# Score matmuls parted around the block matmuls, whole blocks in the last batch, and another order at the program's end

## The chip, the cores and the metric

The kernel runs on one core of a Trainium2 chip. The metric is the device time of one execution in microseconds (us). TensorE (PE) multiplies matrices, with weight loads (PEld) that can run beside it; VectorE (DVE), ScalarE (ACT) and GpSimd (POOL) work on tiles in the on-chip memory; SyncE (SP) issues transfers. All engines take their instructions in program order and wait for each other through semaphores.

## The reference

Eight sequences of 1024 tokens with 256 features go through one layer, all in float32: attention with 16 heads of 16, then a gated feed-forward that mixes each token with the one before it.

```python
x = x + _layernorm(attn(_layernorm(x)))      # softmax(q k^T / 4) v, then w_o
x = x + _layernorm(ffn(_layernorm(x)))
# ffn(x): x_prev = x shifted by one token
# xr = mu_r*x + (1-mu_r)*x_prev ; xk = mu_k*x + (1-mu_k)*x_prev
# sigmoid(xr W_r^T) * ((relu(xk W_k^T)**2) W_v^T)
```

## The kernel before

The work is cut into 16 half batches `u` (8 batches of 2 x 512 queries) of 32 steps `s` each, 512 steps `i` in all. A step handles four heads (`qd`), 512 queries (`hf`) and 128 keys (`kt`). On TensorE a step consists of three things, in this order:

- `scores(i + 1)` (L567): for each of two pairs `p` two matmuls (L577) into the bank pair `PS[p]`, one on rows 0 to 49 and one on rows 64 to 113 of the array, which run side by side. They wait for the exponential of the same pair a step earlier, since it reads the same bank. Each pair has one exponential on ScalarE (L584), 128 x 1024, into `PT`.
- `pump` (L302): a piece of everything else that needs TensorE. That work is cut into blocks. A `Block` is a projection of 128 x 512 or 2 x 128 x 256 outputs in three products of high and low halves, which stand in for float32 (Q, K, V of the next batch: "ahead"; y = w_o, k, r, v of the feed-forward of the half batch before: "behind"). Its contraction over 128 rows is parted into two halves of 64 rows: half 0 on rows 0 to 63, half 1 on rows 64 to 127. `begin` (L255) sends half 0 of a new block beside half 1 of the one before, so that two blocks overlap; each `step_part` (L284) sends half of such a tile, so a tile takes two steps. A `Turn` (`turn`, L243) is four transposes of 128 x 128 and is sent at once. `choose(age)` (L219) takes the first block of each chain that has been ready, and a bank of three that has been free, for `age` steps; the bank freed first is taken first. `pump` sends two pieces in a step where `left` is 0 (steps 0 to 8 of the first half batch).
- `values(i)` (L589): four matmuls (L596; float32, two passes each) on all 128 rows and four column groups of 32, into the accumulator `PO`, after both exponentials of step i.

When a block's last matmul is sent, its `done` queues the work on the other engines; at a `yield REST` it pauses, and goes on one step later. `norm_stats` (L651) computes mean and variance on VectorE and the inverse root on GpSimd (L657, L658), `normed` (L661) applies them. Words name blocks: `Q00` is Q, feature half 0, token half 0; `T10` a transpose of the normalized input, token half 1; `y0 y1`, `z0 z1` (transposes), `k`, `r`, `v` the feed-forward's. The lists `FIRST`, `EVEN`, `ODD` (L828 to L830) give their order; in the last batch, which has none ahead, only "behind" words are left.

Before the loop, `run` (L869) sends the first batch's work: `p_direct` (D and E words, L459) writes the first heads' queries and keys straight into `QS` and `KS`, with a copy on ScalarE (L466) and a subtraction on VectorE (L469). The list `meanwhile` gives small works that are queued after each of these blocks. `keep_warm(n)` (L168) sends n matmuls whose result nobody reads.

After the loop the last half batch's y, z, k, r, v run alone (L978), each on all 128 rows, with fillers (L981) between them: a number in the list of words is so many matmuls that nobody reads. Before each word `rest_no_more` queues all work that is pausing.

Of the kernel before, what the change touches and what calls it, by code (L numbers as in the profile page):

```python
# [56 lines left out]
def sandwich_kernel(nc, x, wpack, consts, out):  # L57
    with ExitStack() as ctx:
# [129 lines left out]
        class Block:  # L188
# [3 lines left out]
            def __init__(self, chain, half, ready, done, queued=(), tokens=None):  # L192
                self.chain, self.half, self.ready, self.done = chain, half, ready, done
                self.seen, self.queued, self.tokens = None, queued, tokens

# [58 lines left out]

        def begin(age):  # L255

            took[:] = 0.0, 0.0
            block = choose(age)
            if isinstance(block, Turn):
                turn(block)  # L260
                return False
            now[:] = block, now[0]
            if now[0] is not None:
                tile[0] = queue(now[0].half(PM[now[0].bank[0]], 0), *now[0].waits[0])
            if now[1] is not None:
                tile[1] = queue(now[1].half(PM[now[1].bank[0]], 1), now[1].token)
            return bool(tile[0] or tile[1])
# [15 lines left out]

        def step_part(age):  # L284


            fresh = not (tile[0] or tile[1])
            if fresh and not begin(age):
                return
            ends = [None, None]  # L290
            limit = [sum(op[0] for op in tile[a]) / 2 - .03 if fresh else 1e9 for a in range(2)]
            emit(*limit, ends)
            if ends[0] is not None:
                now[0].token = ends[0]
            if ends[1] is not None:
                block = now[1]
                now[1] = None
                until_rest(block.done(block.bank[0], PM[block.bank[0]], ends[1]))

        doubled = [False]  # L300

        def pump(left, age=1):  # L302

            for block in waiting:
                if block.seen is None and block.ready() is not None:
                    block.seen = step_now[0]
            need = sum(block.cost for block in waiting) + bool(tile[0] or tile[1])
            step_part(age)
            doubled[0] = not doubled[0] and need > left and step_now[0] % 32 > 9
            if doubled[0] or not left:  # L310
                step_part(age)

# [146 lines left out]
        def p_direct(i, p, n):  # L459
            cols, dst = slice(n * 512, n * 512 + 512), (QS, KS)[i][0]  # L460

            def done(k, m, tok):
                state["qk_read"] = tk["B_read"] = tok
                for a in range(2):
                    rows = slice(64 * a, 64 * a + SHIFT)
                    h = act.op(lambda e, rows=rows: e.activation(dst[rows, p, cols], m[rows, :], ACT.Copy), tok)  # L466
                for a in range(2):
                    rows = slice(64 * a + 32 * i, 64 * a + 32 * i + 16)
                    d = dve.op(lambda e, rows=rows: e.tensor_tensor(dst[rows, p, cols], m[rows, :],  # L469
                                                                    dst[rows, p, cols].bitcast(F32), ALU.subtract), h)  # L470
                free_bank(k, d)
                here.setdefault((0, 0, i, n), []).append(d)
                if meanwhile:
                    meanwhile.pop(0)()
# [91 lines left out]
        steps = [(b, qd, hf, kt) for b in range(B) for hf in range(2) for qd in range(4) for kt in range(8)]  # L566
        def scores(i):  # L567
            b, qd, hf, kt = steps[i]
            if kt == 0:
                maxima(b, qd, hf)  # L570
            for p in range(2):
                waits = [rows_all, *here[b, qd, 0, hf], *here[b, qd, 1, kt // 4]]
# [255 lines left out]
        FIRST = "Q00 K00 V2 K01 V3 Q10 K10 K11 Q01 Q11"  # L828
        EVEN = "W3 T00 T01 y0 y1 Q00 T10 T11 z0 z1 k0 k1 r0 r1 v0 v1 K00 Q01 K01"
        ODD = "y0 y1 z0 z1 k0 k1 r0 r1 v0 v1 Q10 K10 Q11 K11 V0 V1 V2"  # L830
# [82 lines left out]
        def sum_all():  # L913
# [5 lines left out]

        meanwhile[:] = [lambda: ln1_norm(0, 1), lambda: (split_weights(["wv"]), sum_heads()),  # L920
                       sum_all, lambda: None, lambda: split_weights(["wq", "wk"])]
        run("D00 E00 D10 E10 T10 T11 V0 V1 E01 E11")
        flagged, = flagging
        load_xa(1)
        scores(0)
        copier[0] = "dve"

        for u in range(2 * B):
# [6 lines left out]
            for s in range(32):  # L935
                i = step_now[0] = 32 * u + s
                if i + 1 < len(steps):
                    scores(i + 1)
                if s == 12:
                    load_xb(u)  # L940
                rested, resting[:] = resting[:], []
                age = 2 if b + 1 == B and 8 <= s < 20 else 1
                pump(0 if u == 0 and s < 9 else 32 - s, age)
                values(i)
# [32 lines left out]
        idle = xA[:, 0:2, :].rearrange("p t c -> p (t c)")  # L977
        for word in "5 y0 y1 11 z0 z1 8 k0 k1 r0 r1 v0 v1".split():  # L978
            if word.isdigit():
# [3 lines left out]
                continue  # L983
            rest_no_more()
            block(B, 2 * B - 1, word)
# [97 lines left out]
```

## Time and profile before

| | us |
|---|---|
| median of 3 runs | 1304.06 (1302.92 to 1306.53) |
| profiled execution | 1305.91 |
| its span, first to last instruction | 1304.1 |
| TensorE busy | 1273.5 (98%) |
| ScalarE busy | 1056.0 (81%) |
| VectorE busy | 783.0 (60%) |
| GpSimd busy | 271.0 (21%) |
| mean granted TensorE clock | 0.987 |

Times are us from the span's start. TensorE's matmuls are pipelined and a row's length includes the tail, so rows overlap; the distance from one start to the next is what an instruction takes of the engine. A clock of 1.00 is 2.4 GHz, 0.50 is 1.2 GHz. "[0.47 <-DVE xnT L409]" says that the engine stood idle 0.47 us before the row and what ended it.

### The profile page before, as it was taken

What the parts mean: (1) busy time and instruction counts of PE and PEld (TensorE: products, weight loads), DVE (VectorE), ACT (ScalarE), POOL (GpSimd) and SP (SyncE); (2) the same over time, 40 slices, a digit from 0 to 9 for tenths busy, and PEclk for the clock granted to TensorE, in tenths of its full rate; (3) what the DMA queues carried; (4) which work ended last, traced back from release to release, by engine and by line L of the source; (5) the groups of instructions that cost most, each with busy time, mean ns of one, the idle gap of its engine ahead of it and who ended that gap; (6) DMA issues with size and microseconds to landing.
All of it is one profiled execution on the core that took longest, in us unless ns stands there. A gap on an engine that the chain in (4) does not pass through costs nothing.

```text
span 1304.1 us, 25655 instructions
## 1 busy us (share of the span) xinstructions
PE 1273.5 (98%) x10694; PEld 647.4 (50%) x10694; DVE 783.0 (60%) x1726; ACT 1056.0 (81%) x1153; POOL 271.0 (21%) x352
## 2 busy tenths in 40 slices
PE   8999999999999999999999999999999999999995
PEld 5543555455545555455544555455554555444353
DVE  5553656758465774857466584747657474545546
ACT  3588888888888888888888888888888888887831
POOL 1000212222211322222121222113221221212210
PEclk8899999999999999999999999999999999998999
DMA  4256383316612194115733176122942056201000
GB/s 149 60 153 189 86 143 82 98 48 127 116 53 81 52 181 95 50 52 113 132 80 98 50 140 121 45 72 82 162 82 66 28 114 132 55 2 33 1 17 17
DMA packets 61798, 112.72 MB, mean 86 GB/s; under 512 B 6512, under 2 KB 31344, under 8 KB 61616
## 3 DMA queue, kind: packets, MB, share of 16 engines
q1 hardware_dynamic: 61360, 109.60, 37.1%
q8 instruction: 102, 1.67, 0.6%
q10 hardware_dynamic: 288, 1.05, 0.2%
q14 instruction: 48, 0.39, 0.1%
HBM read 68.42 MB, written 41.94 MB: 85 GB/s over the span
## 4 chain that ended last, share of the span: by engine, by line
PE 88%; DVE 7%; ACT 3%; POOL 1%; issue 1%; DMA 0%; POOLq 0%; ACTq 0%
PE O L596 36%; PE S L577 25%; PE M L346 14%; PE M L333 10%; PE M L247 3%; ACT PT L584 2%; DVE sth L653 2%; DVE A L662 1%; POOL rsh L658 1%; PE M L480 1%; DMA A<-w_dram 0%; DVE mvh L655 0%; DVE xB L677 0%; DVE T L616 0%; DVE xnT L409 0%
## 5 line engine op out<-in xcount | busy, mean ns | idle before, releaser
L584 ACT ACTIVATE PT<-S 128x1024 f32<-128x1024 f32 x1024 | 991.4, 1023 | 176.9 <-PE S L577 176.9
L596 PE MATMUL O<-PT,V 128*17 128x512 f32 x4096 | 541.3, 600 | 0.0
L577 PEld LDWEIGHTS S<-QS,KS 50*128 50x128 f32 x2048 | 185.6, 184 | 458.4 <-ACT PT L584 410.9
L577 PE MATMUL S<-QS,KS 50*128 50x512 f32 x2048 | 386.8, 452 | 5.8 <-ACT PT L584 5.6
L657 POOL TENSOR_SCALAR veh<-mvh 128x2 f32<-128x2 f32 x96 | 22.3, 232 | 509.4 <-DVE mvh L655 509.4
L596 PEld LDWEIGHTS O<-PT,V 128*17 128x17 f32 x4096 | 67.9, 95 | 104.9 <-issue 62.9
L796 DVE SCALAR_TENSOR_TENSOR A<-Z,M 128x512 f32<-128x512 f32 x30 | 20.4, 682 | 159.0 <-PE M L346 159.0
L333 PE MATMUL M<-xnT,WH 64*128 64x512 f32 x512 | 112.4, 398 | 0.0
L346 PE MATMUL M<-WH,xnT 64*128 64x256 f32 x512 | 86.7, 284 | 0.0
L346 PE MATMUL M<-WH,cT 64*128 64x256 f32 (+1 forms) x496 | 83.7, 282 | 2.8 <-DVE cT L630 2.1
L371 DVE CAST p<-M 128x512 fp32r<-128x512 f32 x62 | 42.4, 684 | 70.5 <-PE M L333 35.6
L346 PE MATMUL M<-WH,C 64*128 64x256 f32 (+1 forms) x496 | 81.7, 278 | 1.0 <-DVE C L760 1.0
L346 PE MATMUL M<-WH,B 64*128 64x256 f32 (+1 forms) x496 | 81.6, 278 | 0.9 <-DVE B L730 0.9
L719 POOL TENSOR_TENSOR C<-A,C 128x512 fp32r<-128x512 f32 x30 | 38.7, 1291 | 155.1 <-DVE C L371 155.1
L658 POOL TENSOR_TENSOR rsh<-veh,half 128x2 f32<-128x2 f32 x96 | 69.1, 720 | 8.0
L333 PEld LDWEIGHTS M<-xnT,WH 64*128 64x128 f32 x512 | 67.1, 189 | 6.8
L333 PE MATMUL M<-xnT,WL 64*128 64x512 f32 x256 | 70.1, 396 | 0.0
L748 POOL TENSOR_TENSOR scratch<-scratch 128x512 f32<-128x512 f32 x30 | 32.8, 1093 | 177.8 <-DVE scratch L746 177.8
L346 PEld LDWEIGHTS M<-WH,xnT 64*128 64x128 f32 x512 | 68.2, 191 | 0.7 <-DVE xnT L409 0.3
L346 PEld LDWEIGHTS M<-WH,cT 64*128 64x128 f32 (+1 forms) x496 | 65.4, 190 | 4.1 <-issue 2.9
L346 PEld LDWEIGHTS M<-WH,C 64*128 64x128 f32 (+1 forms) x496 | 63.6, 185 | 2.9 <-DVE C L760 1.2
L746 DVE TENSOR_SCALAR scratch<-M 128x512 f32<-128x512 f32 x32 | 22.1, 691 | 70.9 <-PE M L333 62.1
(114 smaller groups left out, 1672.5 us busy)
## 6 DMA issues: line engine op xcount, KB each, us to landing
scr<-p SPq DMA_DIRECT2D x124, 256.0 KB
QS<-scr SPq DMA_DIRECT2D x56, 256.0 KB, 6.1
KS<-scr SPq DMA_DIRECT2D x56, 256.0 KB, 10.5
QS<-scr SPq DMA_DIRECT2D x70, 128.0 KB, 6.0
KS<-scr SPq DMA_DIRECT2D x68, 128.0 KB, 8.1
xA<-x_dram SPq DMA_DIRECT2D x16, 512.0 KB, 7.3
xB<-x_dram SPq DMA_DIRECT2D x16, 512.0 KB, 5.2
out_dram<-xB SPq DMA_DIRECT2D x15, 512.0 KB, 3.1
```

The costliest lines, as they stand in the source:

```text
L247: fn = lambda e, t=t: e.transpose(PM[k][:, t * 128:t * 128 + 128], block.src(t), ident[:, :])
L333: out.append((.216, lambda e, k=k, w=w, v=moving(j, c, rows): e.matmul(m[:, :], w, v, start=(a != 1 and k == 0), stop=(a != 0 and k == 5))))
L346: out.append((.117, lambda e, k=k, t=t, w=w, v=still(i, c, t, rows): e.matmul(m[:, t * 256:t * 256 + 256], v, w, start=(a != 1 and k == 0) ...
L371: return dve.op(lambda e: e.tensor_copy(dst, src), *waits)
L577: fn = lambda e, p=p, a=a, rows=rows: e.matmul(PS[p][:, a, :], KS[qd][rows, p, kt * 128:kt * 128 + 128], QS[qd][rows, p, hf * 512:hf * 512 ...
L584: e_fn = lambda e, p=p: e.activation(PT[i % 2][:, 2 * p:2 * p + 2, :], PS[p][:, :, :], ACT.Exp, scale=SCALE)
L596: fn = lambda e, j=j: e.matmul(PO[32 * j:32 * j + 17, :], V[b % 2][:, kt, 4 * qd + j, :], PT[i % 2][:, j, :], start=(kt == 0), stop=(kt == 7))
L653: toks = [dve.op(lambda e, t=t: e.bn_stats(sth[:, 2 * g + t, :], src(t)), *ready) for t in range(2)]
L657: p = pool.op(lambda e: e.tensor_scalar(veh[:, ts], mvh[:, ts, 1], EPS, None, ALU.add), d)
L658: r = pool.op(lambda e: e.tensor_tensor(rsh[:, ts], veh[:, ts], half[:, 0:2], ALU.pow), p)
L719: tk["xk", u, c] = side().op(lambda e: e.tensor_tensor(C[1][:, cols], A[:, cols], C[0][:, cols].bitcast(F32), ALU.subtract), d)
L748: tk["sq", mt] = k1, r, side().op(lambda e: e.tensor_tensor(r[:, :], r[:, :], r[:, :], ALU.mult), d)
```

## The change

- The main loop calls `scores(i + 1, 0)` before `pump` and `scores(i + 1, 1)` from within it, after the block's matmuls. Transposes that were chosen (`turns`) are sent after that.
- In the last batch (`b + 1 == B`) a block runs `solo`: both halves as one, on all 128 rows, in two steps, and no second block beside it. `age` is 2 there for all steps below 20, and no longer for steps 8 to 19 alone.
- `K00` stands before `T11` in `EVEN`.
- In `p_direct`, the copies of the second token half (E01, E11) go to VectorE.
- Two of the `meanwhile` works get warm-up matmuls: one after E00, two after D10.
- At the end there are 9 and 7 fillers instead of 11 and 8, and before `y1` and `v1` the pausing work of `y0` and `v0` isn't queued first: both pieces' later steps then come turn by turn.

```diff
-        def begin(age):
+        def begin(age, turns):
             took[:] = 0.0, 0.0
-            block = choose(age)
+            block = None if solo[0] and now[0] is not None else choose(age)
             if isinstance(block, Turn):
-                turn(block)
+                turns.append(block)
                 return False
             now[:] = block, now[0]
+            if block is not None and now[1] is None and solo[0]:
+                block.solo = True
+                tile[0] = queue(block.half(PM[block.bank[0]], 2), *block.waits[0])
+                return True
...
-            if ends[0] is not None:
+            if ends[0] is not None and now[0].solo:
+                block = now[0]
+                now[0] = None
+                until_rest(block.done(block.bank[0], PM[block.bank[0]], ends[0]))
+            elif ends[0] is not None:
                 now[0].token = ends[0]
...
-        def pump(left, age=1):
+        def pump(left, age=1, between=None):
...
-            step_part(age)
             doubled[0] = not doubled[0] and need > left and step_now[0] % 32 > 9
-            if doubled[0] or not left:
-                step_part(age)
+            turns = []
+            for k in range(2 if doubled[0] or not left else 1):
+                step_part(age, turns)
+            if between is not None:
+                between()
+            for block in turns:
+                turn(block)
...
-                    h = act.op(lambda e, rows=rows: e.activation(dst[rows, p, cols], m[rows, :], ACT.Copy), tok)
+                    if n:
+                        h = dve.op(lambda e, rows=rows: e.tensor_copy(dst[rows, p, cols], m[rows, :]), tok)
+                    else:
+                        h = act.op(lambda e, rows=rows: e.activation(dst[rows, p, cols], m[rows, :], ACT.Copy), tok)
...
-        EVEN = "W3 T00 T01 y0 y1 Q00 T10 T11 z0 z1 k0 k1 r0 r1 v0 v1 K00 Q01 K01"
+        EVEN = "W3 T00 T01 y0 y1 Q00 T10 K00 T11 z0 z1 k0 k1 r0 r1 v0 v1 Q01 K01"
...
-        meanwhile[:] = [lambda: ln1_norm(0, 1), lambda: (split_weights(["wv"]), sum_heads()),
-                       sum_all, lambda: None, lambda: split_weights(["wq", "wk"])]
+        meanwhile[:] = [lambda: ln1_norm(0, 1), lambda: (split_weights(["wv"]), sum_heads(), keep_warm(1)),
+                       lambda: (keep_warm(2), sum_all()), lambda: None, lambda: split_weights(["wq", "wk"])]
...
-                if i + 1 < len(steps):
-                    scores(i + 1)
+                nxt = i + 1 < len(steps)
+                if nxt:
+                    scores(i + 1, 0)
...
-                age = 2 if b + 1 == B and 8 <= s < 20 else 1
-                pump(0 if u == 0 and s < 9 else 32 - s, age)
+                age, solo[0] = (2 if s < 20 else 1, True) if b + 1 == B else (1, False)
+                pump(0 if u == 0 and s < 9 else 32 - s, age, (lambda: scores(i + 1, 1)) if nxt else None)
...
-        for word in "5 y0 y1 11 z0 z1 8 k0 k1 r0 r1 v0 v1".split():
+        for word in "5 y0 y1 9 z0 z1 7 k0 k1 r0 r1 v0 v1".split():
...
-            rest_no_more()
+            if word not in ("y1", "v1"):
+                rest_no_more()
```

## Rows read from the trace of the kernel before

**Rows 1.** Stretches of the span: start:end length, busy us by engine, PEclk, DMA.
```profile
24.60:31.43 6.83, 6.30 (x44) 5.79 (x45) 3.07 (x7) 2.38 (x4) 0.00 (x0) 0.50 0.49 156
39.05:49.67 10.62, 10.50 (x43) 5.17 (x44) 1.16 (x3) 4.72 (x5) 0.00 (x0) 0.56 0.01 2
1102.90:1252.07 149.17, 145.53 (x1151) 67.09 (x1147) 73.88 (x165) 126.71 (x139) 32.75 (x42) 0.98 0.11 26
1252.07:1275.50 23.43, 19.49 (x66) 11.03 (x62) 15.02 (x42) 1.23 (x2) 6.02 (x12) 0.93 0.07 22
1275.50:1304.10 28.60, 16.98 (x84) 11.85 (x84) 17.14 (x36) 5.84 (x10) 1.87 (x4) 0.89 0.06 19
```

**Rows 2.** Timeline of TensorE, one step with a block: start, length, instruction, count.
```profile
601.33 0.72 PE L577 MATMUL S<-QS,KS 50*128 50x512 f32 x4
601.89 0.63 PE L333 MATMUL M<-xnT,WH 64*128 64x512 f32 x4
...
602.68 1.05 PE L596 MATMUL O<-PT,V 128*17 128x512 f32 x8
603.66 0.73 PE L577 MATMUL S<-QS,KS 50*128 50x512 f32 x4
```

**Rows 3.** Timeline of TensorE, scores and block in a step behind an accumulator copy.
```profile
577.79 0.76 PE L577 MATMUL S<-QS,KS 50*128 50x512 f32 x4
578.38 0.39 PE L333 MATMUL M<-xnT,WH 64*128 64x512 f32 x1
```

**Rows 4.** Timeline of TensorE, the step of T11 in an even half batch.
```profile
525.63 0.79 PE L577 MATMUL S<-QS,KS 50*128 50x512 f32 x4
526.89 0.66 PE L247 MATMUL M<-ident,xA 128*128 128x128 f32 x4 [0.47 <-DVE xnT L409]
```

**Rows 5.** Timeline of TensorE, a half block right behind the last values.
```profile
1252.07 0.38 PE L346 MATMUL M<-WH,C 64*128 64x256 f32 x1
1252.29 0.28 PE L346 MATMUL M<-WL,C 64*128 64x256 f32 x1
...
1252.64 0.28 PE L346 MATMUL M<-WL,C 64*128 64x256 f32 x1
```

**Rows 6.** Stretches: four steps with neither block nor transposes; two steps with transposes.
```profile
1126.53:1134.42 7.89, 7.30 (x52) 1.99 (x49) 5.49 (x17) 7.27 (x9) 2.35 (x5) 1.00 0.01 2
1134.42:1139.09 4.67, 4.67 (x36) 1.78 (x33) 1.75 (x7) 4.01 (x5) 0.00 (x0) 1.00 0.00 0
```

**Rows 7.** Timeline of TensorE, the start.
```profile
23.83 0.19 PE L914 MATMUL S<-gsm,ones 128*1 128x2 f32 x2 [2.12 <-DVE gsm L911]
...
26.19 0.79 PE L480 MATMUL M<-xnT,B 64*128 64x512 f32 x1
...
36.22 0.50 PE L577 MATMUL S<-QS,KS 50*128 50x512 f32 x1
...
39.05 1.71 PE L577 MATMUL S<-QS,KS 50*128 50x512 f32 x4 [1.88 <-ACT PT L584]
```

**Rows 8.** Timeline of ScalarE, the first exponentials.
```profile
37.98 3.85 ACT L584 ACTIVATE PT<-S 128x1024 f32<-128x1024 f32 x4
```

**Rows 9.** Timeline of VectorE and ScalarE's copy, from the last values to y1's norm.
```profile
1252.20 0.60 ACT L613 ACTIVATE On<-O 128x512 f32<-128x512 f32 x1 [1.90 <-PE O L596]
...
1254.68 0.68 DVE L616 STREAM_TRANSPOSE T<-On 128x512 f32<-128x512 f32 x1
...
1256.02 0.73 DVE L662 TENSOR_SCALAR A<-A,mvh,rsh 128x256 f32<-128x256 f32 x2
...
1257.40 0.70 DVE L627 STREAM_TRANSPOSE T<-CC 128x512 f32<-128x512 f32 x1
...
1262.09 0.76 DVE L653 BATCH_NORM_STATS2 sth<-M 128x6 f32<-128x256 f32 x2 [2.60 <-PE M L346]
...
1270.85 0.99 DVE L662 TENSOR_SCALAR A<-M,mvh,rsh 128x256 f32<-128x256 f32 x2 [1.14 <-POOL rsh L658]
```

**Rows 10.** Timeline of TensorE, fillers at the end.
```profile
1264.07 9.60 PE L981 MATMUL S<-xA,ident 128*128 128x512 f32 x22
```

## What the change should do to the time

> **What bounds the kernel now.** I first split the span into stretches and read TensorE's busy share and granted clock in each [rows 1]: the middle of the run and the last batch are full of TensorE work, while the end (52 us, in two rows) has TensorE idle a quarter of the time, and two stretches near the start run at half clock. Then I read one step of the main loop from TensorE's timeline [rows 2]: four score matmuls from 601.33, a tile of block matmuls from 601.89, values from 602.68, the next scores at 603.66. That is 0.56 + 0.79 + 0.98 = 2.33 us without a hole. ScalarE's two exponentials take 1.94 us of it (four in a row 3.85 [rows 8]), so in a step that has a block TensorE sets the pace, and ScalarE has 0.4 us to spare. In a step without one ScalarE sets it: four such steps take 7.89 us, 1.97 each [rows 6]. So I cost a step with a block by TensorE's slots (start to start), a step without by 1.97, the start by clock and waits, the end by its chain of VectorE and GpSimd.
>
> The 0.56 splits as 0.33 for the first score pair and 0.23 for the second; three block slots are 3 x 0.23, and the last has 0.10 more before values, which use another tiling of the array [rows 2].
>
> **Parted scores.** Pair 1's two score matmuls move behind the block; nothing is added. Scores and block halves both work on 64-row tiles, so the order pair 0, block, pair 1, values has the same two changes of tiling as before: 0.33 + 3 x 0.23 + 0.23 + 0.10 + 0.98 = 2.33, no change. Pair 1 then ends about 0.33 + 0.69 + 0.39 = 1.4 us into the step, and the exponential of pair 0 holds ScalarE until about 1.5, so ScalarE isn't starved. On ScalarE's queue a block's own activation (a tanh, two a half batch) now stands before the second exponential; the 0.4 us of slack pays for it. What is gained is the wait of pair 1 for its exponential where that is late: behind an accumulator copy the scores take 0.59 instead of 0.56 [rows 3]. 53 of 387 steps with a block up to the last batch show such an excess, 0.02 to 0.05 each, and 0.47 once when blocks resume after an empty stretch: -2.7 us together. Bounds for a handover from block to score: zero as within a row group now, or 0.10 as after a change of tiling [rows 5]; I take zero, since scores hand to blocks at 0.23 today, and keep the other as a rival.
>
> **K00 before T11.** In every even half batch from the third to the thirteenth (six of them) T11 waits for the bank that T10 has just filled, until VectorE's subtraction ends: released at 526.89 where it could have begun at 526.30 [rows 4], a stall of 0.59. The order of freed banks gives K00 the same bank one step after T10, and its first matmul would be due earlier, at 525.63 + 0.34 = 525.97. The block that feeds VectorE's queue ends 0.23 earlier in its step by the new order, so the release comes at about 526.66: a stall of 0.69. Six times +0.1 is +0.6; bounds -3.5 (stall gone) and +2.0 (release not earlier). K00's stores move by one step on SP's queue, which waits for nothing there.
>
> **The last batch, blocks alone ("solo").** There is only one chain of blocks left, so halves of two blocks pair up only in part. Solo runs a block on all 128 rows in two steps. Counting by the rules of the planner with age 2: in the first half batch V2's second half (2 steps), then V3, y0, y1 to step 7, transposes in 12 and 13, k0 to v1 in 18 to 29; in the second y0, y1 in 4 to 7, transposes in 12 and 13, k0 to v1 in 18 to 29. That makes 34 solo steps, 2 half steps, 4 with a transpose (2.33 each [rows 6]) and 23 empty ones up to the last values.
>
> A solo step has two changes of tiling more: pair 0 (64 rows), block (128), pair 1 (64), values. What a change costs is seen where values hand to a half block: the first slot takes 0.22, the following three 0.35 together [rows 5], so 0.10 of weight load lies open, and rows 2 give 0.10 for the change itself. So a solo step is 0.33 + 0.10 + (6 x 0.117 + 0.10) + 0.10 + (0.23 + 0.10) + 0.10 + 0.98 = 2.75, against 2.33 for a pair. Sum: 34 x 2.75 + 2 x 2.35 + 4 x 2.33 + 23 x 1.97 + 1.7 (last exponential and values) = 154.5, against 149.17 [rows 1]: +5.3. Without any cost of the changes it would be 140.9 (-8.3); I take the dear end, because each change in the trace shows both parts. The old 149.17 holds a stretch at half clock (0.98 on average), where y0 was sent before its operand was there; at age 2 the operand is ready some 2 us ahead, so I count none.
>
> The Trainium skill ("TensorE: Matmul & The Clock Gate", on the array's architecture and queue depths) says that TensorE's queue can pull weight loads ahead of matmuls in flight. By that the 0.10 of load would be hidden; the first slots in rows 5 show that behind a change of tiling it was not, so this sum stays with the rows, and the rule has its place among the rivals. "TensorEngine Tiling (Array Packing)", key properties, says that a change of mode drains the engine and a change of tile alone does not; it gives no price, and it speaks against solo and for the parted scores.
>
> **The start.** TensorE stood idle 2.12 us before 23.83, and the clock was at half (0.50) from 24.60 to 31.43 [rows 1, 7]. The three warm-up matmuls (two passes each, 0.43 a pass, as the fillers at the end [rows 10]) fit into that hole and the one at 20 us, so they cost nothing; if they overran, D10 would wait 0.2. At half clock an E10 matmul lasts 0.79 instead of 0.39 [rows 3, 7]; its tile of six slots goes from 2.5 to 1.4 with its tail, and K's copies and E01 follow it: -1.4 (bounds 0 and -3.4, half of the stretch). E01's and E11's copies leave ScalarE for VectorE, where their subtractions already queue: four more copies of about 0.7; their readers come four steps later. The first scores are there at 36.22 + 0.5, and the exponential began at 37.98 only behind those copies [rows 7, 8]: -1.2. Then TensorE waited 1.88 us for both exponentials [rows 7], the clock fell again, and the first two steps took 10.62 us at 0.56 [rows 1]. Now pair 0 waits for one exponential and a block follows, a hole of under 1 us; two double steps at full clock are 2 x (2.33 + 0.70) = 6.1: -4.5. Together -7.1. If a fall stays in either place, only -2.6 is sure.
>
> **The end.** v1 is done two steps before the loop ends. Now its work stands in VectorE's way: the accumulator copy (0.60 after the last values at 1252.07) ends at about 1252.8, the transpose starts at 1254.68, 1.9 later, and v1's normalization begins 1.4 before the second transpose at 1257.40 [rows 9]. Without both y0's operand, there at 1262.09 - 2.60 = 1259.5 [rows 9], comes 3.1 earlier, 4.3 to 4.4 us after the last values, as the five fillers (10 passes, 4.3 [rows 10]) end; so no idle and no half clock, and VectorE waits 1.9 instead of 2.60 for y0's twelve slots: -0.7. Then the norms of y0 and y1: now each waits twice for GpSimd, 1.14 each [rows 9], in series, 13.4 us until both are normalized. Turn by turn, y0's wait is covered by y1's work and the other way round: 8.9 of VectorE work plus 0.4 (y1's matmuls) and 0.4 (the last wait) = 9.8, -3.6. Nine fillers (7.7) end 1 us before the transposes. After them v0 and v1 likewise wait twice 1.14, of which 0.2 remains: -2.1. The first output transfer is issued 0.6 later, still 1.5 before the second. Seven fillers (6.0) still end before k0's operand. Together -9.5; lower bound -6 if the clock falls between, upper -10.
>
> **Sum.** -2.7 + 0.6 + 5.3 - 7.1 - 9.5 = -13.4. The profiled execution spans 1304.1 us (1305.91 with what lies around it, 1.85 above the median 1304.06, within the three runs). From the median: 1290.7, so 1291.
>
> **Rivals.**
> - Weights are loaded ahead through solo's changes: 34 x 2 x 0.10 = 6.8 less, 1284. For it: loads overlap everywhere inside one tiling; against it: rows 5. Chance 0.12. (This is the skill's rule above.)
> - The clock falls again, at the start (hole of 1.4 us before E01, 0.7 before the first step) or at the end: +4.5 to +5, 1296. The shortest hole before a fall so far was about 2 us. Chance 0.15.
> - Slower: a score behind a block doesn't get its weights early, since its wait for the exponential stands between them in the queue. At 0.10 in each of some 390 steps that is +39, 1330. It decides from 0.034 a step (13.4 / 390). Against it: the same wait stands before pair 1 today, which starts without a hole. Chance 0.07.
> - It comes out even, 1304: solo costs more (2.95 a step) and half of the start's gain stays out. Chance 0.08.
> - The forecast: 0.58.
>
> A measurement of this kernel tells 0.3% (3.9 us) from no change. Faster by more: forecast, weights ahead, nearly all of the clock case: 0.84; within: 0.08; slower: 0.08. The range: from 1282 (weights ahead, with K00's stall gone) to 1300 (clock case with K00's dear end).
>
> **What would show it.** In a step of the middle: pair 0 to block 0.33, last block slot to pair 1 0.23, step 2.33; if the step is 2.43, the handover rival is right. In the last batch steps with a block at 2.75. K00 waiting about 0.7 for VectorE behind T10. Clock 1.00 from 24.6 to the end, the third step starting at about 42.6 instead of 49.67. At the end: statistics of y1 before y0's normalization, the transposes some 16 us after the last values instead of 23.4, and 26.5 from there to the end instead of 28.6. What would make it wrong is above all the price of solo: 0.1 a step is 3.4 us.

## The result, and the profile after

The changed kernel takes 1298.62 us (median of 6 runs, 1295.87 to 1299.68) beside 1304.61 for the kernel before (6 runs); the ratio is 0.995, with a 95% interval from 0.9937 to 0.9963. A second set of five runs gave 1299.57 (e4 below); over all eleven the median is 1299.3. So the change brings 5 to 6 us. The forecast was 13: the direction and the range hold, but the gain is less than half of it.

The profiled execution of the changed kernel took 1295.87 us with a span of 1294.1, the fastest of all eleven; that of the kernel before took 1305.91, 1.3 above its median. From trace to trace the gain is 10.0 us, from median to median 5.3. Both numbers have to be explained.

I cut both spans at the same three places of the program: the values of the third step, of the last step ahead of the last batch, and of the last step of all. The four stretches of the changed kernel (start:end length, busy us of TensorE, its weight loads, VectorE, ScalarE and GpSimd with counts, granted clock, DMA share, GB/s):

```profile
0.00:44.85 44.85, 39.19 (x245) 24.39 (x245) 27.22 (x63) 19.27 (x27) 6.34 (x12) 1.00 0.34 111
44.85:1095.94 1051.09, 1047.54 (x9159) 499.72 (x9157) 652.27 (x1426) 908.24 (x971) 223.47 (x283) 1.00 0.45 98
1095.94:1251.12 155.18, 150.90 (x975) 58.81 (x973) 78.47 (x175) 130.79 (x140) 35.76 (x46) 1.00 0.10 25
1251.12:1294.10 42.98, 32.71 (x142) 19.55 (x142) 28.17 (x67) 7.07 (x12) 6.85 (x13) 0.94 0.07 25
```

In the kernel before, the same four take 51.75, 1050.16, 149.17 and 53.02. So the start gives 6.9 and the end 10.0, the loop costs 0.9 and the last batch 6.0. The loop's 0.9 is within what traces of the old loop differ by: e1 and e2 below run it unchanged and take 1049.57 and 1051.68 for it (in e2 two single steps of 3.35 and 3.18 us hold 1.8 of that). The changed loop takes 1051.1 to 1051.3 in nine traces.

**Start.** The two stretches that were at half clock [rows 1] are not: here is the first again, and the first two steps, 6.11 us instead of 10.62.

```profile
24.60:31.43 6.83, 5.07 (x58) 4.45 (x60) 4.16 (x9) 4.01 (x7) 0.00 (x0) 1.00 0.48 154
36.66:42.77 6.11, 6.11 (x44) 3.10 (x44) 3.86 (x7) 4.70 (x5) 0.00 (x0) 1.00 0.00 0
```

TensorE's timeline (start, length, instruction, count, [idle before <- what ended it]) has the 2.12 us before the sums [rows 7] down to 0.20. Two holes of nearly 1 us stay:

```profile
23.79 0.19 PE L931 MATMUL S<-gsm,ones 128*1 128x2 f32 x2 [0.20 <-DVE gsm L928]
...
30.45 0.49 PE L497 MATMUL M<-xnT,B 64*128 64x512 f32 x1 [0.97 <-DVE KS L486]
...
36.66 0.50 PE L594 MATMUL S<-QS,KS 50*128 50x512 f32 x2 [0.89 <-ACT PT L601]
```

**A step of the loop.** TensorE's timeline of a step with two half blocks:

```profile
599.71 0.50 PE L594 MATMUL S<-QS,KS 50*128 50x512 f32 x2
600.05 0.28 PE L360 MATMUL M<-WH,xnT 64*128 64x256 f32 x1
...
600.75 0.40 PE L594 MATMUL S<-QS,KS 50*128 50x512 f32 x2
601.08 1.05 PE L613 MATMUL O<-PT,V 128*17 128x512 f32 x8
602.06 0.73 PE L594 MATMUL S<-QS,KS 50*128 50x512 f32 x4
```

Pair 0 to block 0.34, block to pair 1 without a hole, pair 1 to values 0.33, values 0.98: 2.35 us, as [rows 2] but for 0.02.

**K00 behind T10.** In an even half batch K00 now waits where T11 waited [rows 4]:

```profile
519.13 0.50 PE L594 MATMUL S<-QS,KS 50*128 50x512 f32 x2
520.17 0.73 PE L347 MATMUL M<-xnT,WH 64*128 64x512 f32 x4 [0.54 <-DVE xnT L423]
```

The block comes 1.04 after the scores, of which 0.70 is waiting.

**A step of the last batch with a whole block.** Rows of 128 in the block's form (128*128) where the loop has 64:

```profile
1104.38 0.50 PE L594 MATMUL S<-QS,KS 50*128 50x512 f32 x2
1104.81 0.39 PE L360 MATMUL M<-WH,xnT 128*128 128x256 f32 x1
1105.03 0.28 PE L360 MATMUL M<-WL,xnT 128*128 128x256 f32 x1
...
1105.71 0.50 PE L594 MATMUL S<-QS,KS 50*128 50x512 f32 x2
1106.14 1.05 PE L613 MATMUL O<-PT,V 128*17 128x512 f32 x8
1107.12 0.51 PE L594 MATMUL S<-QS,KS 50*128 50x512 f32 x2
```

0.43 + 0.90 + 0.43 + 0.98 = 2.74. In the loop the hand-overs from pair 0 and from pair 1 take 0.34 and 0.33; here both take 0.43, and the block's first slot takes 0.22 where the next takes 0.12.

**End.** VectorE's timeline, to be held against [rows 9]:

```profile
1252.87 0.71 DVE L633 STREAM_TRANSPOSE T<-On 128x512 f32<-128x512 f32 x1 [2.02 <-ACT On L630]
...
1258.30 0.76 DVE L670 BATCH_NORM_STATS2 sth<-M 128x6 f32<-128x256 f32 x2 [1.84 <-PE M L360]
1258.98 0.30 DVE L672 BATCH_NORM_AGGREGATE mvh<-sth 128x2 f32<-128x6 f32 x2
1259.74 0.76 DVE L670 BATCH_NORM_STATS2 sth<-M 128x6 f32<-128x256 f32 x2 [0.46 <-PE M L360]
...
1265.86 0.70 DVE L679 TENSOR_SCALAR A<-xB,mvh,rsh 128x256 f32<-128x256 f32 x2
1267.16 0.73 DVE L679 TENSOR_SCALAR A<-xB,mvh,rsh 128x256 f32<-128x256 f32 x2 [0.61 <-POOL rsh L675]
```

The transpose starts as soon as the accumulator is copied, y1's statistics follow y0's at once, and of the four waits for GpSimd only 0.61 us is left.

### The profile page after: what moved, and what is told of

It reads as the page before. It is cut to its first block, busy times and chain, and to the rows that moved or that the text cites. A ratio compares the mean times of both kernels' runs of the same rounds, so it can differ in the third digit from the quotient of the medians.

```text
span 1294.1 us, 25293 instructions
## 1 busy us (share of the span) xinstructions
PE 1270.3 (98%) x10514; PEld 602.5 (47%) x10514; DVE 786.1 (61%) x1729; ACT 1065.4 (82%) x1149; POOL 272.4 (21%) x353
## 4 chain that ended last, share of the span: by engine, by line
PE 89%; DVE 6%; ACT 3%; issue 1%; POOL 1%; DMA 0%; ACTq 0%
PE O L613 36%; PE S L594 25%; PE M L360 14%; PE M L347 10%; PE M L247 2%; ACT PT L601 2%; DVE sth L670 1%; DVE A L679 1%; PE M L497 1%; DMA A<-w_dram 0%; DVE xB L694 0%; POOL rsh L675 0%; DVE xnT L423 0%; DVE mvh L672 0%; PE S L1001 0%
## 5 line engine op out<-in xcount | busy, mean ns | idle before, releaser
L601 ACT ACTIVATE PT<-S 128x1024 f32<-128x1024 f32 x1024 | 1006.1, 1026 | 172.3 <-PE S L594 171.9
L594 PE MATMUL S<-QS,KS 50*128 50x512 f32 x2048 | 462.6, 453 | 4.6 <-ACT PT L601 4.6
L594 PEld LDWEIGHTS S<-QS,KS 50*128 50x128 f32 x2048 | 207.9, 183 | 460.4 <-ACT PT L601 351.2
L360 PE MATMUL M<-WH,xnT 64*128 64x256 f32 (+1 forms) x504 | 83.1, 278 | 0.3 <-DVE xnT L423 0.3
L360 PE MATMUL M<-WH,C 64*128 64x256 f32 (+1 forms) x464 | 78.9, 280 | 0.9 <-DVE C L777 0.9
L360 PE MATMUL M<-WH,cT 64*128 64x256 f32 (+1 forms) x464 | 79.1, 280 | 0.0
L360 PEld LDWEIGHTS M<-WH,xnT 64*128 64x128 f32 (+1 forms) x504 | 65.1, 186 | 1.2 <-DVE xnT L423 0.5
L647 POOL TENSOR_TENSOR cT<-T,cT 128x512 fp32r<-128x512 f32 x31 | 46.5, 1499 | 81.0 <-DVE cT L385 80.6
L633 DVE STREAM_TRANSPOSE T<-On 128x512 f32<-128x512 f32 x64 | 44.8, 700 | 30.7 <-ACT On L630 30.7
L360 PEld LDWEIGHTS M<-WH,B 64*128 64x128 f32 (+1 forms) x464 | 61.0, 186 | 3.4 <-issue 2.0
```

What stands on the lines that cost most here:

```text
L360: out.append((.117, lambda e, k=k, t=t, w=w, v=still(i, c, t, rows): e.matmul(m[:, t * 256:t * 256 + 256], v, w, start=(a != 1 and k == 0) ...
L594: fn = lambda e, p=p, a=a, rows=rows: e.matmul(PS[p][:, a, :], KS[qd][rows, p, kt * 128:kt * 128 + 128], QS[qd][rows, p, hf * 512:hf * 512 ...
L601: e_fn = lambda e, p=p: e.activation(PT[i % 2][:, 2 * p:2 * p + 2, :], PS[p][:, :, :], ACT.Exp, scale=SCALE)
L633: d = dve.op(lambda e: e.transpose(at[:, :], On[:, :]), d, tk.get(("T", g % 2)), split_of["wr"])
L647: d = side().op(lambda e: e.tensor_tensor(cT[1][:, cols], at[:, :], cT[0][:, cols].bitcast(F32), ALU.subtract), d)
```

## The experiments

The theory I started from: the prediction's terms are right one by one and add up, and what is missing in the median is a fall of the clock in most executions. Its rivals: the parts disturb each other, or one of them costs more than its term. Medians of the kernel before beside these runs were 1304.2 to 1304.7.

**e1, the start's edits alone** (copies of E01 and E11 on VectorE, warm-up matmuls; the rest as before).

> The kernel before with the start's edits alone (three warm-up matmuls, the copies of E01 and E11 on VectorE). Theory A (the traces' stretches hold, the parts add up): third step of the loop at 42.8 instead of 49.7, the rest unchanged, so 6.9 us less, about 1297.7 against 1304.6. Theory B (what was gained at the start in one profile is given back in most executions, because the clock falls there all the same): the median moves by 3 us or less and the granted clock differs between executions.

Measured 1300.58 (12 runs), ratio 0.997 (0.996 to 0.998): -4.1 us, between the two. In its trace the clock still falls once at the start, from 38.4 to 45.2 us.

**e2, the end's edits alone** (9 and 7 fillers, y1 and v1 without `rest_no_more`).

> The kernel before with the end's edits alone (9 and 7 fillers, norms turn by turn). v1 stays in VectorE's way and the fall of the clock at y0 stays, so of the end's 10.0 us only the two reorderings are left: 3.6 + 2.1 = 5.7 us less, about 1299 (theory A). Theory B: fewer fillers let the clock fall in between in most executions, 2 us less or nothing.

Measured 1299.98 (5 runs), ratio 0.9967 (0.9954 to 0.998): -4.7. The end takes 46.0 us instead of 53.0, 7.0 less where 5.7 was expected: before y0's first matmul TensorE stands idle as long as in the kernel before, but there the clock then fell to 0.50 (1260.2 to 1263.6), and in e2 it stayed at 1.00. The row before (first) and in e2:

```profile
1259.63 0.36 PE L346 MATMUL M<-WH,cT 128*128 128x256 f32 x1 [2.11 <-DVE cT L630]
```
```profile
1257.32 0.36 PE L346 MATMUL M<-WH,cT 128*128 128x256 f32 x1 [2.11 <-DVE cT L630]
```

The other 3.0 us of the end's gain in the whole change come from the new plan of the last batch, which leaves no work of v1 for the end. The trace of e2 has something I hadn't looked for, the last batch by the old plan at full clock:

```profile
1102.82:1248.76 145.94, 142.31 (x1148) 65.84 (x1146) 74.69 (x166) 127.71 (x140) 31.81 (x40) 1.00 0.11 27
```

e1's trace has 145.87 for it. The 149.17 of the profile before [rows 1] holds a half-clock stretch from 1185.1 to 1192.0 that neither has, though all three wait in the same place for y0's operand (0.67 in e1 and e2; before that 0.39 or 0.40 for an exponential). The row in the kernel before:

```profile
1183.97 0.39 PE L346 MATMUL M<-WH,cT 64*128 64x256 f32 x1 [0.68 <-POOL cT L630]
```

So the last batch's plan costs 155.2 - 145.9 = 9.3 us, not 6.0.

**e3, the loop's edits alone** (parted scores, K00's place, whole blocks in the last batch).

> The kernel before with the loop's edits alone (parted scores, K00 before T11, solo blocks and age 2 in the last batch). Theory A: +0.9 up to the last batch, +6.0 in it, -3.8 at the end since v1 is done earlier and y0 meets no idle engine: +3 us, about 1307.7. Theory B (solo blocks cost nothing net, the loss lies in the granted clock of some executions): within 1 us of before in its profile's stretches.

Measured 1309.06 (5 runs), ratio 1.0036 (1.0023 to 1.0049): +4.4. The loop half of the change is a loss. The three parts add: -4.1 - 4.7 + 4.4 = -4.4, beside -5.1 for the whole in the same runs.

**e4, the changed kernel again.**

> The changed kernel once more. Its first profile was its fastest execution (1295.9; six executions from 1295.9 to 1299.7). Theory A (the rest of the forecast's miss beside the four terms of the trace is granted clock): executions near 1299 have 0.995 to 0.997 and those near 1296 0.998 or more, and a profile of a slow one has a stretch at 0.50 which the first profile has not. Theory B: equal clocks, and the difference lies in transfers or elsewhere.

Measured 1299.57 (5 runs). The profiled one of them took 1299.15, 3.28 above the first trace, and it has what was expected: one more half-clock stretch. A window of e4, and the same one of the first trace below it:

```profile
37.20:44.03 6.83, 6.83 (x28) 3.59 (x27) 2.37 (x4) 3.36 (x4) 0.00 (x0) 0.50 0.00 0
```
```profile
37.20:44.03 6.83, 6.83 (x54) 3.84 (x54) 3.69 (x6) 5.04 (x6) 0.00 (x0) 1.00 0.04 5
```

28 matmuls instead of 54 in the same 6.83 us; the third step's values come at 48.00 instead of 44.85, and from there on the two traces differ by less than 0.2 us. It is the same program: the two holes of almost 1 us stand in both. Eight traces have these two holes (the first, e1, e4, and e6 to e10 below): five show such a stretch at 0.50 behind them, three (the first, e7, e10) don't. Of the eleven executions two have a mean clock of 0.998 or more (1295.87 and 1296.43); the other nine have 0.994 to 0.997 and take 1297.9 to 1300.9.

**e5, two more fillers in those holes.**

```diff
-                       lambda: (keep_warm(2), sum_all()), lambda: None, lambda: split_weights(["wq", "wk"])]
+                       lambda: (keep_warm(2), sum_all()), lambda: None, lambda: (keep_warm(1), split_weights(["wq", "wk"]))]
...
         scores(0, 0, 1)
+        tk["On_read"] = pe.op(lambda e: e.matmul(PO[:, :], On[:, 0:128], On[:, :], start=True, stop=True),
+                              on_set, tk["acc_free"])
```

> The changed kernel, with one more idle matrix product behind the first token block of the start (where TensorE stood 0.97 us before line 497) and one more, into the accumulator, behind the first scores (where it stood 0.88 us before line 594). Theory A: the changed kernel's median lies 3.3 us above its best execution because in most executions the granted clock falls once to 0.50 for some 6.8 us behind these two holes (in the repeat it was 0.52 over 37 to 43 us, in the other profile 1.00); with the holes filled it does not fall: every execution at a mean clock of 0.998 or more, within 1295.5 to 1297, median 1296, and the third step starts at 42.8 us. Theory B: the fall does not come from these holes: the spread stays, median 1299.3, clock 0.994 to 0.999, as in the repeat.

Measured 1297.64 (8 runs). Four of eight executions are at 0.998 or more and take 1296.1 to 1296.8, the others up to 1300.0. Theory A holds in part; some falls stayed.

**e6, both score pairs ahead of a whole block, in the last batch alone.**

```diff
+                last = b + 1 == B
...
-                    scores(i + 1, 0)
+                    scores(i + 1, *((0, 1) if last else (0,)))
...
-                pump(0 if u == 0 and s < 9 else 32 - s, age, (lambda: scores(i + 1, 1)) if nxt else None)
+                pump(0 if u == 0 and s < 9 else 32 - s, age, (lambda: scores(i + 1, 1)) if nxt and not last else None)
```

> The changed kernel, but in the last batch both score pairs stand ahead of the block; everything before that batch stays. Theory A: a step with a whole block on all rows is 2.75 us instead of 2.35 because TensorE changes its tiling three times in it, and each change exposes some 0.10 us of draining and 0.10 us of a weight load; with the scores together one change goes, the 34 such steps take 2.54 us, the last batch 155.2 - 34 x 0.21 = 148.1 us, and the kernel 1292.2 against 1299.3. Theory B: the whole block itself costs it (its twelve products run 0.4 us longer than two halves side by side), steps stay at 2.75 us, the kernel at 1299.3; it would lose further if late exponentials come back in the last batch, by under 1 us.

Measured 1293.38 (4 runs), -5.9 against the changed kernel; the last batch takes 149.02 instead of 155.18.

```profile
1112.55 0.73 PE L594 MATMUL S<-QS,KS 50*128 50x512 f32 x4
1113.21 0.39 PE L360 MATMUL M<-WH,cT 128*128 128x256 f32 x1
...
1113.91 0.28 PE L360 MATMUL M<-WH,cT 128*128 128x256 f32 x1
1114.12 1.05 PE L613 MATMUL O<-PT,V 128*17 128x512 f32 x8
1115.10 0.73 PE L594 MATMUL S<-QS,KS 50*128 50x512 f32 x4
```

0.66 + 0.91 + 0.98 = 2.55: one change of tiling less is 0.20 us. Theory A, to 0.01 in 31 of the 34 steps; the other three, the first behind an empty stretch, stay at 2.72 to 2.75 (their scores take 0.86 instead of 0.66), so the batch is 0.9 above 148.1. Parting the scores and whole blocks, two edits of one change, work against each other.

**e7, no whole blocks in the last batch.**

```diff
-                age, solo[0] = (2 if s < 20 else 1, True) if b + 1 == B else (1, False)
+                age, solo[0] = (2 if s < 20 else 1, False) if b + 1 == B else (1, False)
```

> The changed kernel, but in the last batch the blocks stay halved and side by side as in the rest of the loop (blocks still wait two steps up to step 20, one after it); the last block's second half then lies behind the last values. Theory A: a step that holds two halves takes 2.35 us, so the last batch takes 17 + 12 + 4 + 4 + 4 such steps x 2.36 + 4 x 2.33 with transposes + 18 x 1.98 without a block = about 143.6 us instead of 155.2, and the end is 3.8 us longer (42.0 to 45.8): 1299.3 - 11.6 + 3.8 = 1291.5. Theory B: the whole blocks were needed for the chain of the last pieces, and the end loses as much as the batch gains: 1299 or more.

Measured 1295.85 (5 runs; 1290.77 in the profiled one).

```profile
1095.93:1239.43 143.50, 140.80 (x1143) 61.57 (x1141) 73.92 (x161) 128.47 (x140) 32.07 (x40) 1.00 0.11 27
1239.43:1289.00 49.57, 35.82 (x156) 22.48 (x154) 33.97 (x83) 7.07 (x12) 7.73 (x16) 0.93 0.07 22
```

The batch is theory A's to 0.1 us (143.6 expected). The end loses 6.6 instead of 3.8: v0's and v1's work stands before the transpose on VectorE again, as in [rows 9], so that this starts 5.65 us after the last values instead of 1.75; TensorE then stood idle for 3.49 us, and the clock fell from 1251.2 to 1254.6. Set against the first trace, 1295.87 - 11.7 + 6.6 is this execution's 1290.8. The median lies between the theories: the two executions at a mean clock of 0.997 took 1290.77 and 1291.49, the three at 0.992 and 0.993 took 1295.85 to 1297.24, and no trace shows where those three lost the clock. The end's loss suggests that whole blocks are worth something, but only for the last ones (e10 tests it).

**e8, scores never parted** (whole blocks and K00's new place kept).

> The changed kernel with both score pairs ahead of the block everywhere; its whole blocks in the last batch, K00's place, the start and the end stay. Theory A: parting bought 2.7 us in the loop (the late exponentials of steps 1, 9, 17 and 25 of each half batch, hidden) and cost 0.21 us in each of the 34 steps with a whole block: loop from the third step to the last batch 1096.9 + 2.7 = 1099.6, last batch 148.1, kernel 1294.9. Theory B: in the loop parting also cost as much in the other steps (0.01 to 0.03 us in steps with a block of values or a mixed tile) as it won: loop 1097 or below, kernel 1292.

Measured 1293.74 (4 runs). Loop 1052.17, last batch 149.05. In the loop parting is worth 1.1 us here, between the theories; over all it loses.

**e9, K00 back behind v1.**

```diff
-        EVEN = "W3 T00 T01 y0 y1 Q00 T10 K00 T11 z0 z1 k0 k1 r0 r1 v0 v1 Q01 K01"
+        EVEN = "W3 T00 T01 y0 y1 Q00 T10 T11 z0 z1 k0 k1 r0 r1 v0 v1 K00 Q01 K01"
```

> The changed kernel with K00 in the even half batches back behind v1; all else stays. Theory A: K00's new place costs more than the 0.6 us of the forecast, because in the first half batch the blocks then no longer pair (steps 18 to 28: two more steps with half a block, two empty ones fewer, +0.6 us between values 2 and 31), and because in six later half batches the values of step 11 wait 0.32 us longer and get only 0.11 us of it back; so the stretch from the third values to those of step 447 is 1051.1 - 0.6 - 6 x 0.21 = 1049.2 us. Theory B: parting the scores makes those steps longer, not K00's place: 1050.5 or above.

One execution, 1295.76 with the fall at 36.9 us in it. The loop in two windows (third values to those of step 31, and on to step 447), e9 first, then the changed kernel, then e1, which has the old loop:

```profile
48.01:118.00 69.99, 69.39 (x522) 30.73 (x520) 35.85 (x74) 57.69 (x61) 3.82 (x5) 1.00 0.62 167
118.00:1095.77 977.77, 976.31 (x8638) 467.98 (x8636) 615.78 (x1352) 850.54 (x911) 219.93 (x278) 1.00 0.42 93
```
```profile
44.85:115.53 70.68, 70.30 (x523) 31.78 (x521) 35.92 (x74) 57.80 (x61) 3.81 (x5) 1.00 0.62 166
115.53:1095.94 980.41, 977.24 (x8639) 467.94 (x8637) 616.35 (x1352) 850.44 (x911) 219.66 (x278) 1.00 0.43 93
```
```profile
48.57:118.65 70.08, 69.48 (x523) 31.23 (x521) 36.01 (x74) 56.25 (x61) 3.81 (x5) 1.00 0.61 167
118.65:1098.14 979.49, 976.55 (x8638) 498.60 (x8636) 615.85 (x1351) 842.76 (x911) 219.62 (x278) 1.00 0.43 93
```

K00's new place costs 0.69 + 2.64 = 3.3 us, more than theory A said. In each of the six half batches step 11 is about 0.55 longer and step 13 0.11 shorter. With K00 where it was, T11 waits less than in the kernel before:

```profile
520.76 0.79 PE L594 MATMUL S<-QS,KS 50*128 50x512 f32 x4
521.79 0.66 PE L247 MATMUL M<-ident,xA 128*128 128x128 f32 x4 [0.24 <-DVE xnT L423]
```

**e10, four steps of whole blocks at the very end.**

```diff
-                age, solo[0] = (2 if s < 20 else 1, True) if b + 1 == B else (1, False)
+                age, solo[0] = (1, hf == 1 and s >= 28) if b + 1 == B else (1, False)
```

> The changed kernel, but in the last batch a block waits one step after its inputs throughout (two up to step 20 before), and blocks are whole only from step 28 of the last half batch on. Two blocks come out whole then, and the last one still ends ahead of the last values. Theory A: last batch 2 x 2.75 + 42 x 2.36 + 4 x 2.33 + 15 x 1.98 + 1.9 = 145.5 us instead of 155.2, end as in the changed kernel (42.96 from the last values on): 1299.3 - 9.7 = 1289.6. Theory B: with one step of waiting, products reach the head of TensorE's queue while their inputs are still being made (as in the one step of 3.94 us of the kernel before), so that the batch takes 149 us or more: 1293 or above.

Measured 1289.39 (4 runs), ratio 0.9901 (0.9871 to 0.993). Theory A's time, but with some luck: the batch takes 1.2 more than its count and the end 0.7 more, which by the same base would be 1291.5; two of the four executions, the traced one among them, are at a mean clock of 0.998.

```profile
1096.10:1242.83 146.73, 142.44 (x1154) 62.84 (x1152) 77.13 (x171) 128.76 (x140) 34.17 (x43) 1.00 0.11 27
1242.83:1286.50 43.67, 32.73 (x142) 19.54 (x142) 29.46 (x72) 7.07 (x12) 7.98 (x15) 0.95 0.07 24
```

**e11, what these runs pointed to, put together** (e10 + e9 + e5, scores together in the last whole-block steps).

> The kernel of e10_four_solo, with K00 at its old place, the two idle products of e5_fill at the start, and the scores together in the last steps. If the parts add: from the changed kernel's 1299.3 (median of its two sets) -9.7 for the last batch, -0.2 for the scores of the last steps, -1.9 for K00, -1.7 for the clock at the start = 1285.8 (1284.5 to 1288). If the last batch's gain is lost at the end: 1293.

Measured 1287.37 (6 runs, 1285.16 to 1290.65), ratio 0.9883 (0.986 to 0.9907): within the range given, 1.6 above the sum.

**e12, the start without the change's own fillers.**

```diff
-        meanwhile[:] = [lambda: ln1_norm(0, 1), lambda: (split_weights(["wv"]), sum_heads(), keep_warm(1)),
-                       lambda: (keep_warm(2), sum_all()), lambda: None, lambda: split_weights(["wq", "wk"])]
+        meanwhile[:] = [lambda: ln1_norm(0, 1), lambda: (split_weights(["wv"]), sum_heads()),
+                       lambda: sum_all(), lambda: None, lambda: split_weights(["wq", "wk"])]
```

> The changed kernel without the start's new idle products (behind sum_heads and ahead of sum_all); the copies on VectorE, which shorten the waits there, stay. Theory A: it is the idle products that keep the clock: without them it falls to 0.50 at 24.6 us for 6.8 us, as in the kernel before (24.6 to 31.4) and in two of the experiments without the start's edits, the third step's values start 3 us later (48 instead of 44.9, or later yet with a second fall), and the median is 1302.5. Theory B: the waits that the copies shorten are what mattered, the idle products only fill them: 1299.3.

Measured 1298.76 (10 runs), the changed kernel's time, as theory B had it. Its trace is mixed: a 2.1 us hole at 23.4 again, and half-clock stretches of 3.4 us from 28.2 and, behind a wait of 2.05 us for a transfer, from 7.7, but none at 37; the third step's values come at 47.5, near theory A's 48. That the copies are what helps is not shown, since no run has the fillers without the copies. By themselves these fillers gain nothing that can be measured; by the mean clocks (0.994 to 0.998) most executions lose the clock somewhere with them or without.

**e13 and e14, two further fillers at the start,** on e5 and on e11. `turn` calls the next work of `cold` ahead of its transposes; `warm_half` sends half a filler.

```diff
-        keep_warm(3)
+        keep_warm(4)
...
+        cold[:] = [lambda: None, warm_half]
         run("D00 E00 D10 E10 T10 T11 V0 V1 E01 E11")
```

> The kernel of e5_fill with two more idle products at the start: a fourth before line 899, where TensorE stood 0.8 to 1.3 us, and half a one before the second group of transposes, where it stood 0.53 us. Theory A: what is left of the spread (four of the eight executions of e5_fill were at a mean clock of 0.998 or more and 1296.1 to 1296.8, the others at 0.996 and 0.997 and up to 1300.0) comes from falls behind the holes that e5_fill left at the start: nearly all executions at 0.998 or more, median 1296.3. Theory B: the falls that are left lie elsewhere, or do not follow such holes: median 1297.6 and the same spread.

> The kernel of e11_best with the same two additions. Theory A: median at the best execution of e11_best, 1285.2 (up to 1286.3), instead of 1287.4. Theory B: 1287.4, with executions up to 1290.7 as there.

e13: 1296.75 (6 runs, 1295.95 to 1298.5). All six are at 0.998 or 0.999, so theory A holds for the clock; the median is 0.45 above it, and one execution of 1298.5 at 0.999 has another cause, which I didn't find. e14: 1285.70 (4 runs, 1285.15 to 1285.83), all at 0.999, ratio 0.9863 (0.9847 to 0.988): theory A. It is the fastest version here, 13.6 us below the changed kernel. Its four stretches:

```profile
0.00:45.03 45.03, 43.02 (x253) 25.96 (x253) 27.22 (x63) 19.27 (x27) 6.34 (x12) 1.00 0.34 110
45.03:1092.78 1047.75, 1045.84 (x9159) 499.04 (x9157) 651.41 (x1426) 908.04 (x971) 223.45 (x283) 1.00 0.43 98
1092.78:1239.48 146.70, 142.42 (x1155) 62.99 (x1153) 76.86 (x170) 128.72 (x140) 34.18 (x43) 1.00 0.11 27
1239.48:1283.40 43.92, 32.73 (x142) 19.52 (x142) 29.69 (x73) 7.07 (x12) 7.98 (x15) 0.96 0.07 24
```

## Why the prediction was right or wrong

Three steps failed: that holes of about 1 us at the start leave the clock alone (3.4 us of the median), that K00 costs 0.1 a half batch (0.6 forecast, 3.3 measured), and that one profile with falls of the clock in it can be the base of the sum (1.3 us of the median, and 3.3 us in the price of the last batch).

**The start, -7.1: right for one execution, wrong for the median.** From the trace before to the trace after it is -6.9. But in the repeat's trace the clock falls at 37 us behind holes of 0.97 and 0.89, +3.2 us, and by the mean clocks nine of eleven executions have such a loss. I had put that at 0.15, on the ground that the shortest hole before a fall had been about 2 us. That was a rule made from one trace, and it failed both ways. The same trace has the fall at 1185.1, behind holes of 0.39 and 0.68 us; behind holes of 0.97 and 0.89 the clock fell in some executions and not in others; and behind the same 2.11 us ahead of y0 it fell in the kernel before and not in e2. What the runs show, by their mean clocks, is that with four holes filled all ten executions were at 0.998 or more (e13, e14), with two filled six of fourteen (e5, e11), in the changed kernel itself two of eleven. What decides between executions stays open. The rival "the clock falls again, 1296" was the case that came true for most executions; its 1296 is 3.3 below the median of 1299.3, since the terms' errors in the traces (3.4, see the sum) come on top.

**The last batch, +5.3: step price and count right, the base wrong.** The steps take 2.73 to 2.76 for a forecast 2.75, and 34 of them came, with 155.2 for 154.5. The step that failed is the comparison with 149.17. I saw that this stretch was at 0.98 and left it; its fall of the clock costs 3.3 us that the two other traces of the same plan don't have (145.9 in e1 and e2). Set against those, the cost is +9.3. The sum then took the other error along: it was made against a profile and set off from a median 1.85 below it, as if that profile's extra fall were in every run. The rival "weights are loaded ahead" is out: the first slot behind a change takes 0.22, and removing one change gave back 0.20 a step (e6): the two score pairs take 0.66 together where they took 0.43 + 0.43.

**K00 before T11, +0.6: the wrong alternative.** The wait I worked out for K00, 0.69, is what came: 0.70. But I compared it with T11's old 0.59, although I had written that the block now ends 0.23 earlier in its step and the release comes earlier. Without the move that would have helped T11 instead: its idle row falls from 0.47 to 0.24 (e9). So the move costs 0.44 in each of six half batches, where I had put 0.1; and in the first half batch, which I hadn't counted at all, its order leaves blocks unpaired (step 27 has half a block where it had none), another 0.7. Together +3.3. In the traces this is the largest of the errors.

**Parted scores, -2.7: near, by another way.** With K00 back, the loop is 1.8 us below that of e1 (-0.1 and -1.7 in the two windows), 2.4 below the kernel before's and 3.9 below e2's. The hand-over is free, as taken: pair 0 to block 0.34, block to pair 1 without a gap. The 0.47 where blocks resume is gone (the step that took 2.81 takes 2.34). But the late exponentials give only 0.01 to 0.03 in four steps of a half batch (1, 9, 17 and 25), and a few others (7, 8, 24, 26, 30) get 0.01 to 0.02 longer, as means over the later half batches, which nothing in my sum had; why they do is open. Some 1.3 us of the gain is T11's shorter wait. The rival at 1330, a score behind a block starting 0.10 late, is out.

**The end, -9.5: right.** 53.02 to 42.98, -10.0, each part where it was put: counted from the start of the last values, statistics of y0 at 7.2 us where they were at 11.0, y1's behind them, the transposes at 16.8 where they were at 24.4. (The working's 8.9 + 0.4 + 0.4 is 9.7, not 9.8.) e2 shows that 3 us of this belong to the last batch's plan, which clears VectorE; without that plan (e7) they come back, and 3.6 more, with a fall of the clock.

**The sum.** In the traces: -6.9 + 0.9 + 6.0 - 10.0 = -10.0, where -13.4 was forecast; the 3.4 between them are 3.0 in the loop, 0.7 in the last batch and 0.2 at the start, less 0.5 at the end. Most of the loop's 3.0 is K00; its old length is known to some 1 us only. In the medians 1.3 goes because the kernel before was profiled above its median, and 3.4 because the changed one was profiled below its own: -10.0 + 1.3 + 3.4 = -5.3. The Trainium skill ("TensorEngine Tiling (Array Packing)", key properties) says that a change of mode drains the engine. The traces agree: 0.20 us a change here, the weight load behind it included (e6).

## What to carry to other kernels

Before a stretch of one trace serves as the base of a sum, compare its clock and length with those of a second execution: here one fall of the clock in the base and one missing in the result moved the answer by more than any term's error. When one edit shifts a release and another changes who waits for it, price the second against the kernel with the first edit in it, not against the old one. Two edits that are each good can meet in one step: parted scores are free between blocks of the same tiling and cost 0.20 us a step next to a whole block.

## What the runs showed of the hardware that was not expected

- One program, with the same holes on TensorE, had its clock at 0.50 for 6.83 us in one execution (e4) and at 1.00 in another; in the changed kernel these took 1299.15 and 1295.87 us. The length of the hole did not settle it: 0.68 us or 2.11 us of idle TensorE stood before a fall in one trace and before none in another. Filling four at the start held the mean clock at 0.998 or more in ten executions out of ten.
- A change of the tiling cost 0.20 us, the hand-over and the first weight load together: a step takes 2.75 us with two extra changes, 2.55 with one, 2.35 with none.
- Parted scores made some steps with neither a late exponential nor a stall 0.01 to 0.02 us longer, as means over a dozen half batches. That stays unexplained.
